# A four-layer graph network on one core: edge offsets found by an index search, and the order of the first loads

## What is computed

```python
src = concatenate([_s, _d, arange(3125)]); dst = concatenate([_d, _s, arange(3125)])
order = argsort(dst, stable=True); src, dst = src[order], dst[order]

# layer 0: h = x + segment_sum(x[src], dst); relu(h @ W1 + b1) @ W2 + b2 + x @ Wres + bres
# layer 1: two rounds of x + mean over edges, each through two matrices and a relu
# layer 2: dinv = rsqrt(segment_sum(edge_weight, dst) + 1); four times
#          h = xc @ W_phi.T; neigh = segment_sum(norm * h[src], dst) + dinv * dinv * h
#          xc = xc + 0.1 * tanh(xc @ A.T + neigh + bias)
# layer 3: relu(segment_sum((x @ W + b)[src] + edge_feats @ We + be, dst))
# each layer: x = layernorm(x + layer(x))
```

## Time and profile before

| | us |
|---|---|
| median of 3 runs | 1227.33 (1222.25 to 1231.22) |
| profiled execution, time | 1227.0 |
| its span in the trace | 1225.2 |
| granted TensorE clock, mean | 0.943 |
| busy: TensorE / VectorE / ScalarE / GpSimd | 1089.1 / 556.4 / 297.7 / 103.3 |
| prologue: up to the first instruction of the build | 115.6 |

### The profile page before, as it was taken

How to read it: one execution, slowest core, us unless ns; L and a number is a source line. 1 busy time by engine, 2 the same in 40 slices (tenths; PEclk the granted TensorE clock), 3 DMA queues, 4 the chain that set the end, 5 groups by cost and what they waited for, 6 DMA issues and landing times.

```text
span 1225.2 us, 25749 instructions
## 1 busy us (share of the span) xinstructions
PE 1089.1 (89%) x10720; PEld 634.8 (52%) x10720; DVE 556.4 (45%) x1066; ACT 297.7 (24%) x579; POOL 103.3 (8%) x92
## 2 busy tenths in 40 slices
PE   5013699999988999999999999999999999999898
PEld 4013566667665445454545644556455465546454
DVE  1866788898945333552322321233123123453324
ACT  2013688998932001011000000000000001212200
POOL 4883000000000000000000000001000000000000
PEclk9556599998999999999999999999999999999999
DMA  5421356677777557467776798749976599663951
GB/s 153 142 61 45 162 240 277 281 300 313 312 319 317 204 215 308 177 272 297 266 312 228 278 379 318 295 156 369 381 301 261 204 360 382 253 241 125 428 207 29
DMA packets 39238, 311.56 MB, mean 254 GB/s; under 512 B 10873, under 2 KB 13161, under 8 KB 17298
## 3 DMA queue, kind: packets, MB, share of 16 engines
q1 hardware_dynamic: 27983, 298.70, 62.1%
q0 software_dynamic: 11200, 12.09, 3.6%
HBM read 245.45 MB, written 65.24 MB: 254 GB/s over the span
## 4 chain that ended last, share of the span: by engine, by line
PE 81%; issue 6%; POOL 5%; DVE 5%; ACT 1%; DMA 1%; DVEq 0%; ACTq 0%; POOLq 0%
PE ps L1153 43%; PE ps L1143 15%; PE ps L1264 7%; PE ps L1239 6%; PE ps L1100 4%; POOL arena L436 3%; POOL arena L444 3%; PE ps L1056 2%; PE ps L1113 1%; PE ps L1052 1%; DVE arena L643 1%; PE ps L1005 1%; DVE arena L711 1%; DVE arena L709 1%; DVE arena L712 1%
## 5 line engine op out<-in xcount | busy, mean ns | idle before, releaser
L1153 PE MATMUL ps<-arena 125*128 125x500 f32 (+1 forms) x700 | 267.7, 538 | 0.0
L1153 PE MATMUL ps<-arena,parts_even 125*128 125x500 f32 (+1 forms) x700 | 267.6, 538 | 0.0
L1153 PEld LDWEIGHTS ps<-arena,parts_even 125*128 125x128 f32 x700 | 122.9, 189 | 127.4 <-issue 127.4
L1153 PEld LDWEIGHTS ps<-arena 125*128 125x128 f32 x700 | 122.9, 189 | 127.4 <-issue 127.4
L1143 PE MATMUL ps<-arena 125*128 125x500 f16 (+2 forms) x700 | 141.0, 353 | 5.0 <-issue 4.4
L1264 PE MATMUL ps<-arena 64*128 64x52 f16 (+1 forms) x6500 | 120.3, 181 | 27.2 <-DVE arena L643 20.7
L1264 PEld LDWEIGHTS ps<-arena 64*128 64x128 f16 x6500 | 101.3, 96 | 67.5 <-issue 38.2
L927 ACT ACTIVATE arena<-ps 128x400 f16<-128x400 f32 (+1 forms) x195 | 115.3, 591 | 35.3 <-PE ps L1264 28.6
L913 ACT ACTIVATE XT<-ps 128x500 f32<-128x500 f32 (+1 forms) x49 | 26.5, 541 | 400.4 <-PE ps L1113 400.3
L638 DVE TENSOR_TENSOR arena<-arena 128x4224 f16<-128x4224 f16 (+2 forms) x52 | 116.3, 2236 | 0.0
L759 DVE TENSOR_TENSOR arena<-ps,dinv 125x512 f32<-125x512 f32 (+1 forms) x28 | 17.8, 635 | 198.1 <-PE ps L1100 198.1
(11 more groups left out here) (177 smaller groups left out, 840.5 us busy)
## 6 DMA issues: line engine op xcount, KB each, us to landing
arena<-weight_mats SPq DMA_DIRECT2D x24, 3250.0 KB, 11.5
arena<-weight_mats SPq DMA_DIRECT2D x24, 3000.0 KB, 11.0
arena<-count_mats SPq DMA_DIRECT2D x18, 3125.0 KB, 11.7
weight_mats<-arena SPq DMA_DIRECT2D x13, 3125.0 KB, 14.3
count_mats<-arena SPq DMA_DIRECT2D x13, 1562.5 KB, 5.9
arena<-weight_mats SPq DMA_DIRECT2D x4, 1625.0 KB, 6.4
arena<-weight_mats SPq DMA_DIRECT2D x4, 1500.0 KB, 6.2
arena<-count_mats SPq DMA_DIRECT2D x3, 1562.5 KB, 6.4
```

Of the source, the lines that this page charges most:

```text
L1153: ins = t.matmul(o, xs[:, k, :], rhs, start=(k == 0), stop=(k == NC - 1))
```

## The change

The block of 256 edges stays, but a table of five of them is one window now: `BT4` = 5, `WIN` = 1280, `NBLK` = 405 (404 before).

- **One stretch for a partition instead of a block for a node.** Only the first node of each partition is compared with the block heads: five VectorE comparisons of 81x125 instead of four of 101x3125, five one-column matmuls instead of 100. `win_at` is the first edge of the window. GpSimd gathers one window of 1280 `dst` for each partition with a single indirect DMA instead of 25 of 256.
- **A search instead of a count.** VectorE turns the window into f32, with 32 node numbers behind it so that every value is found, and looks up eight node numbers at once with `max_index`, which gives the first position of each. Four searches (`FINDS`) cover the 25 nodes. Pointers come in groups of eight nodes (`FIND`) instead of five, so GpSimd waits for `ptr_ok` at nodes 0, 8, 16 and 24.
- **The searches stand ahead** of the order check, the x and the weights' work on VectorE; the counting before stood behind them.
- **Order of the loads.** SP loads heads, pairs and edge weights, then waits for `table_ok`, stores the table, waits for `win_in`, and only then issues `here`, `after` and x. The weight matrices, bias columns and rows, 18 DMAs, are issued by ScalarE behind a wait for `table_out`.
- One more flag: a window that ends before the partition's last node.

```diff
-BT4 = 4
+BT4 = 5
 BLOCK = 256
-NBLK = -(-(EDGES + SLOTS) // BLOCK)
+WIN = BT4 * BLOCK
+NBLK = BT4 * -(-(EDGES + SLOTS) // WIN)
+FIND = 8
+FINDS = -(-NC // FIND)
...
         @block.sync
...
             sp.dma_start(t_w, edge_w.rearrange("(p t) -> p t", t=TILES)).then_inc(table_in, 16)
+            sp.wait_ge(table_ok, 1)
+            sp.dma_start(table.rearrange("(p t) c -> p t c", t=TILES), t_rows).then_inc(table_out, 16)
+            sp.wait_ge(win_in, 16)
+            flat = dst_blocks.rearrange("a b -> (a b)")
+            for i, t in enumerate((here, after)):
+                sp.dma_start(t, flat[i:i + 128 * ORDERED].rearrange("(p t) -> p t", p=128)).then_inc(order_in, 16)
             sp.dma_start(Xn[:, :, :], x.rearrange("(p c) f -> p c f", c=NC)).then_inc(x_in, 16)
-            for k, t in Wn.items():
-                sp.dma_start(t[:, :], w[k]).then_inc(w_in, 16)
...
         @block.gpsimd
...
             pool.wait_ge(blk_ok, 1)
-            for c in range(NC):
-                nc.gpsimd.indirect_dma_start(dblk[:, c, :], None, dst_blocks,
-                                             bass.IndirectOffsetOnAxis(blki[:, c:c + 1], 0)).then_inc(dblk_in[c // CG], 16)
+            nc.gpsimd.indirect_dma_start(win_i, None, dst_blocks.rearrange("(a b) c -> a (b c)", b=BT4),
+                                         bass.IndirectOffsetOnAxis(win_ati[:, :], 1)).then_inc(win_in, 16)
 
             table_v = table.rearrange("(a b) t -> a (b t)", b=SLOTS)
             pool.wait_ge(table_out, 16)
             for c in range(NC):
-                if c % CG == 0:
-                    pool.wait_ge(ptr_ok, c // CG + 1)
+                if c % FIND == 0:
+                    pool.wait_ge(ptr_ok, c // FIND + 1)
...
         @block.vector
...
+            dve.wait_ge(first_ps, 1)
+            link(v.tensor_scalar(win_at[:, :], ps[0:NP, 0, 0:1], -1.0, 0.0, ALU.add, ALU.max))
+            link(v.tensor_scalar(win_at[:, :], win_at[:, :], float(NBLK - BT4), float(BLOCK), ALU.min, ALU.mult))
+            v.tensor_copy(win_ati[:, :], win_at[:, :]).then_inc(blk_ok, 1)
+
             dve.wait_ge(table_in, 32)
             v.tensor_copy(t_rows[:, :, 0:2], t_pairs)
             v.tensor_copy(t_rows[:, :, 2], t_w).then_inc(table_ok, 1)
...
             dve.wait_ge(consts, 2)
+            dve.wait_ge(win_in, 16)
+            link(v.tensor_copy(win[:, 0:WIN], win_i))
+            for i in range(FINDS):
+                cs = slice(FIND * i, min(FIND * i + FIND, NC))
+                n = cs.stop - cs.start
+                link(v.max_index(found[:, i, :], dval[:, FIND * i:FIND * i + FIND], win))
+                link(v.tensor_scalar(ptrf[:, cs], found[:, i, 0:n], win_at[:, :], float(EP - SLOTS), ALU.add, ALU.min))
+                v.tensor_scalar(ptr3[:, cs], ptrf[:, cs], 3.0, None, ALU.mult)
+                v.tensor_scalar(ptr8[:, cs], ptrf[:, cs], float(FE), None, ALU.mult).then_inc(ptr_ok, 1)
+
             dve.wait_ge(order_in, 32)
...
-            for i in range(NC // CG):
-                cs = slice(CG * i, CG * i + CG)
-                dve.wait_ge(dblk_in[i], 16 * CG)
-                link(v.tensor_tensor(cmp2[:, cs], dblk[:, cs], d_c[:, cs].to_broadcast([NP, CG, BLOCK]), ALU.is_lt))
-                link(v.tensor_reduce(ptrf[:, cs], cmp2[:, cs], AX, ALU.add))
...
         @block.scalar
         def _(act):
             s = nc.scalar
+            act.wait_ge(table_out, 16)
+            for k, t in Wn.items():
+                act.dma_start(t[:, :], w[k]).then_inc(w_in, 16)
+            for i, k in enumerate(WT):
+                act.dma_start(raw_w[:, i, :], w[k]).then_inc(w_in, 16)
...
             for a in range(BT4):
                 pe.wait_ge(before_ok, a + 1)
-                for c in range(NC):
-                    ins = t.matmul(ps[0:NP, 0, c:c + 1], before[:, a, c, :], blk_ones,
-                                   start=(a == 0 and c == 0), stop=(a == BT4 - 1), skip_group_check=True)
+                ins = t.matmul(ps[0:NP, 0, 0:1], before[:, a, :], blk_ones, start=(a == 0), stop=(a == BT4 - 1))
```

More of the change, by code:

```diff
@@ L26 @@
 I32 = mybir.dt.int32
+U32 = mybir.dt.uint32
 ALU = mybir.AluOpType
@@ L244, in build_program @@
         blk_ok = sem("blk_ok")
-        dblk_in = [sem(f"dblk_in{i}") for i in range(NC // CG)]
+        win_in = sem("win_in")
         ptr_ok = sem("ptr_ok")
```

72 lines of the change are left out of this document (31 added, 41 removed).

## The result

| | before | changed kernel |
|---|---|---|
| median, us | 1227.54 (1222.25 to 1231.22) | 1209.47 (1208.4 to 1210.95) |
| ratio to before, 95% interval | | 0.986 (0.9826 to 0.9893) |
| span of the profiled execution | 1225.2 | 1206.6 |
| last record ready (L601, now L597) | 107.15 | 80.54 |
| first instruction of the build | 115.56 | 88.72 |

A forecast was written before the change was run, and what follows sets the result against it. GpSimd's back-to-back indirect DMAs were taken to bound the prologue. With the chain moved to x, ScalarE's queue and VectorE, the last record comes at 73.6 instead of 107.15: 33.5 us off 1227.0 gives 1193.5 us, range 1183 to 1209.

The forecast's parts named there:

- The window: Prologue: GpSimd's one gather of dst issued at about 7.7 us, 6.5 us to land, there at 14.2 (12.0 to 16.7).
- The search: VectorE, prologue: 1.6 us per search over 1312 elements, first pointers at 17.5, last of four rounds at 25.0, hidden.
- one-pass price: VectorE's search streams the data once past all eight values: 1.6 us a search.
- eight-pass rival: VectorE's search costs one pass per value, 12.2 us each; nearly no gain, 1224 us; seven in a hundred.
- The table: Prologue: store of the table issued ahead of x, 6.7 us to land, `table_out` at 18.0, at worst 22.0.
- GpSimd: Prologue: 25 table gathers start at 18.0 instead of 60.08 and take 42.8 us; last rows land at 60.8.
- x: Load of x on SP behind the table and window: 12.4 us, landed at 32.4; `round_ok` not before 41.4.
- ScalarE's queue: 18 DMA issues before ScalarE's x copies take 8.1 to 20.7 us; `round_ok` at 35.3 to 47.9, middle 41.6; 42.5 taken.
- rule of turns between the queues: DMA engines alternate between SP's and ACT's queues, so ScalarE's issues would not stick behind x; sum about 1 us lower.
- VectorE behind it: After `round_ok`, VectorE needs 9.1 us to the records' start at 51.6, then 22.0 for five groups, ending at 73.6.
- The shift: Everything behind the last record, build included, moves earlier as a block; build still starts 8.4 us after that record.
- rival of the build that gives some back: TensorE's slow clock lasts longer into the build, costing 5 to 8 us, 1200 us; one in fourteen.

The follow-up runs named there:

- three paddings: Changed kernel with 48 early, 95 early or 95 late extra TensorE instructions ahead of the build's loop: 1196.6, 1198.1 and 1198.8 us.

## Why the prediction was wrong

Step by step:

- **The window.** Forecast: issued at 7.7, landed at 14.2 (12.0 to 16.7). Measured: 5.70 and 17.2. The landing of 6.5 us was mis-sized; it took 11.6. The issue came 2 us early. I priced it by the median landing of gathers of 125 KB, but with 625 KB on 125 rows the width counts, and the run with 128 rows took 4.3. That the earlier trace rows showed a share of 0.30 for the 125 partitions of x should have been carried over to the other transfer of 125 partitions.
- **The search.** Forecast 1.6 us; measured 0.09 + 1.52. The one-pass price of the Trainium skill's page "Vector Engine (DVE) Microarchitecture Reference", section 3.9, is borne out by this trace, and the eight-pass rival is refuted.
- **The table.** Forecast `table_out` at 18.0; measured 18.0, by luck: two errors cancel, stored 2.2 us earlier, and 8.9 us on the way instead of 6.7.
- **GpSimd.** Forecast: begins at 18.0, last rows at 60.8. Measured: 21.2 and about 64; not on the chain, as forecast.
- **x.** This is one of the two terms that failed in the prologue. Forecast: 12.4 us at the rate of the earlier trace rows, with 2 for the copies of `dst`, landed at 32.4. Measured: issued at 18.07, landed at 37.6, 19.5 us. The rate was that of x almost alone, and x was not alone: from 18 to 24 us the DMA share is 0.83 to 0.89. The trace of before had the better row: x issued at 4.87 and, by the wait that the earlier trace rows shows, landed at 22.9, 18.0 us later:

```profile
4.87 0.34 SPq L341 DMA_DIRECT2D x_buf<-in_x  x1
```

With the 9.0 us behind it, x alone sets `round_ok` to 46.6, 4.1 us later than the 42.5 taken.
- **ScalarE's queue.** This is the other. Forecast: 18 issues in 8.1 to 20.7 us, middle taken; `round_ok` at 42.5. Measured: 23.2 us, beyond SP's row, and `round_ok` at 50.4, 3.8 us beyond what x alone gives; with the queue emptied of these issues 3.1 of them went. I had let the rule of turns between the queues, from the Trainium skill's page "DMA: Bandwidth & Descriptors", pull the value down. The trace disagrees with what I made of it: in a queue of their own, the issues of ScalarE took 5.91 and 5.30 us while x was loading from SP's, and they shrank to at most 2.97 when x was cut in two. A row that shows a stall should have been kept as the likely value, not as the upper end.
- **VectorE behind it.** Forecast 9.1 us to the records and 22.0 for them; measured 9.3 (50.49 to 59.76) and 20.8. Right in kind; the records took 1.2 us less, so of the 7.9 us by which `round_ok` was late 6.9 were left at their end.
- **The shift.** "Everything behind it should shift as a block": this was the second failure, and it is as large as the first, 8.0 us. The rival of the build that gives some back had the size (5 to 8 us), but little of the reason. It had the slow clock at the build's start last longer in the build; it did, by 4.4 us, but the way from the build's first instruction to the first store took 19.2 us (19.6 before), and the first pair behind it 1.5 us more. The other 6.4 us were spread over the pairs behind it: 0.12 us or more at a pair's start, and four more dips of 1.2 us. I had asked what the removed matmuls cost, and not what their absence does to the program behind them: 95 matmuls fewer ahead of a loop are also 95 instructions fewer. Why that matters to the loop stays open.

The mechanism of the gain was right: the block gathers left the chain and the chain moved to x, ScalarE's queue and VectorE. With the 95 instructions put back, 1198.1 us, the prologue's miss of 7 us stays, and the time is in the range.

## What to carry to other kernels

When an edit removes instructions ahead of a hot loop, compare a period of that loop before and after; if it moved by a tenth of a microsecond though nothing in it changed, pad the program back and time that before judging the edit; here that was worth 9 to 12 us of 1209. A load moved to another engine's queue puts all that its issues wait for ahead of that engine's work, so price it by the worst stall that the trace shows for such issues. And look at how many partitions a DMA has: here 128 rows took 4.3 us where 125 took 11.6.

## What the runs showed of the hardware

- **A 125-row indirect gather of 625 KB landed after 11.6 us, one of 128 rows after 4.3.** The DMA share was 0.32 and 0.21 in the last 4 us of the former, with the end of one store beside it. By the Trainium skill, "DMA: Bandwidth & Descriptors", section on why a DMA increments its semaphore by 16, the number of engines is the largest up to 16 that divides the slowest dimension of both sides, so 5 for 125 rows and 16 for 128. A share of 0.32 and the two landings agree with it; which engines worked no view here shows.
- **DMA issues on one engine's queue were held up while another's large load was under way**: 5.91 and 5.30 us for two of ScalarE's small loads beside x on SP, 6.87 and 3.66 in the kernel before with the new load order, and at most 2.97 with x cut in two. In x's own queue it was no better: 3.55, 4.90 and 3.75 us.
- **TensorE's granted clock dipped to 0.50 for about 3.4 us at the start of a pair**, and each dip cost 1.2 us. TensorE had been without work for 1.15 us before, but so it had in the pairs that did not dip; with five extra matmuls there it did not dip once in 11 pairs, in either kernel.
- **A loop with 95 instructions fewer ahead of it took 0.12 us more a turn** and had more dips: 9 to 12 us of 1209 in all, by three paddings, each against its own before (1196.6, 1198.1 and 1198.8 us).
